# Two conditional token layers on one core: expert tables built in groups of four, and a rearranged start and end

## The reference

```
out_nr  = gelu(x @ w1_nr  + b1_nr)  @ w2_nr  + b2_nr            # condition 0
out_tsr = gelu(x @ w1_tsr + b1_tsr) @ w2_tsr + b2_tsr           # condition 1
h       = gelu(x @ w1_sr + b1_sr)          # 256 -> 512, condition 2
out_sr  = gelu(h @ w2_sr + b2_sr) @ w3_sr + b3_sr
x1 = layernorm(x + out_of_the_condition) * gamma + beta

hid = gelu(x1 @ down_W.T + down_b)                               # 256 -> 64
hid = hid @ expert_W[domain].T + expert_b[domain] + domain_emb[domain]
y   = layernorm(hid @ up_W.T + up_b + x1) * ln_gamma + ln_beta
```

## Time and profile before

| | us |
|---|---|
| median of 3 runs | 279.01 (278.82 to 284.55) |
| the profiled execution, its own time | 278.94 |
| its span, first to last instruction | 277.2 |
| TensorE busy | 262.2 (95%) |
| VectorE, ScalarE, GpSimd busy | 208.6, 207.6, 150.0 |
| mean granted TensorE clock | 0.991 |

### The profile page before, as it was taken

One profiled execution on the slowest core, in us unless ns is written; L12 is line 12 of the kernel. 1 busy time (PEld: TensorE's weight loads), 2 busy tenths in 40 slices (PEclk: granted clock), 3 DMA queues, 4 the chain that ended last, 5 costly groups with the idle time before them and its releaser, 6 DMA issues.

```text
span 277.2 us, 8503 instructions
## 1 busy us (share of the span) xinstructions
PE 262.2 (95%) x2163; PEld 242.8 (88%) x2164; DVE 208.6 (75%) x724; ACT 207.6 (75%) x490; POOL 150.0 (54%) x171
## 2 busy tenths in 40 slices
PE   8999999999999998899999999999999999999850
PEld 6688989999999997799999999999999999999640
DVE  7886241545944945989898899989889999898882
ACT  3577597687687686688888878888888888887720
POOL 3232554555656656555566655656665555565563
PEclk9999999999999999999999999999999999999996
DMA  6471210111131121132332424233242423231122
GB/s 176 132 248 38 50 41 21 23 41 25 35 78 39 37 76 42 34 95 66 85 85 66 104 67 129 69 85 85 66 104 66 124 68 92 78 93 39 59 78 79
DMA packets 44030, 20.93 MB, mean 76 GB/s; under 512 B 37783, under 2 KB 42182, under 8 KB 44008
## 3 DMA queue, kind: packets, MB, share of 16 engines
q1 hardware_dynamic: 41428, 15.21, 22.4%
q0 software_dynamic: 1584, 4.33, 4.2%
q10 hardware_dynamic: 996, 1.13, 1.5%
HBM read 11.96 MB, written 8.65 MB: 74 GB/s over the span
## 4 chain that ended last, share of the span: by engine, by line
PE 84%; DVE 7%; issue 3%; ACT 1%; DMA 1%; POOLq 0%; POOL 0%; DVEq 0%; SPq 0%; ACTq 0%
PE ps_h L1024 19%; PE ps_u L1152 11%; PE ps_z L1101 11%; PE ps_d L1167 6%; PE ps_z L1106 6%; PE ps_t L1123 5%; PE ps_u L1059 5%; PE ps_z L1059 5%; PE ps_z L1089 4%; PE ps_t L1217 3%; PE ps_u L991 3%; PE ps_t L1220 3%; PE ps_t L1218 3%; DMA per_unit_sb<-in_per_unit 1%; DVE n L694 1%
## 5 line engine op out<-in xcount | busy, mean ns | idle before, releaser
L464 POOL TENSOR_TENSOR h_lo<-h,h_hi 128x256 fp32r<-128x256 f32 (+1 forms) x75 | 69.6, 928 | 78.1 <-ACT h L850 78.0
L469 POOL TENSOR_TENSOR rs<-ve,minus_half 128x4 f32<-128x4 f32 x36 | 40.5, 1124 | 32.8 <-DVE ve L670 32.5
L850 ACT ACTIVATE h_hi<-ps_h,per_feature_sb 128x256 fp32r<-128x256 f32 x84 | 38.1, 479 | 23.0 <-PE ps_h L1024 22.2
L658 DVE BATCH_NORM_STATS2 st<-ps_z 128x6 f32<-128x256 f32 x66 | 24.9, 417 | 29.8 <-PE ps_z L1106 29.8
L486 POOL DMA_INDIRECT out<-o,out_rows_now x33 | 35.1, 1064 | 7.9 <-issue 6.2
L889 ACT ACTIVATE yt<-ps_t,per_feature_sb 128x256 f32<-128x256 f32 x66 | 34.0, 573 | 6.3 <-PE ps_t L1123 6.3
L857 ACT ACTIVATE zn<-ps_z,nm,rs 128x256 f32<-128x256 f32 x66 | 33.5, 562 | 6.2 <-DVE nm L674 6.2
L850 ACT ACTIVATE h<-ps_h,per_feature_sb 128x256 f32<-128x256 f32 x84 | 38.0, 481 | 0.0
L1152 PE MATMUL ps_u<-table_hi,stack 128*128 x132 | 35.9, 302 | 0.1
L1152 PE MATMUL ps_u<-table_lo,stack_hi 66*128 x132 | 33.0, 281 | 0.0
L1101 PE MATMUL ps_z<-last_hi,h_hi 128*128 (+1 forms) x132 | 32.6, 280 | 0.3 <-ACT h_hi L850 0.3
(11 more groups left out here) (156 smaller groups left out, 691.1 us busy)
## 6 DMA issues: line engine op xcount, KB each, us to landing
x<-in_x_feat SPq DMA_DIRECT2D x130, 64.0 KB
out<-o SPq DMA_DIRECT2D x65, 64.0 KB, 2.0
last_sb<-in_last_w SPq DMA_DIRECT2D x1, 768.0 KB, 4.7
out<-o,out_rows_now POOLq DMA_INDIRECT x33, 2.8
w_sr_sb<-in_w_sr SPq DMA_DIRECT2D x1, 512.0 KB, 4.5
w_sr_sb<-in_w_sr ACTq DMA_DIRECT2D x1, 512.0 KB, 5.8
w_two_sb<-in_w_two SPq DMA_DIRECT2D x1, 512.0 KB, 5.3
per_unit_sb<-in_per_unit ACTq DMA_DIRECT2D x1, 325.0 KB
```

What stands on the lines that cost most here:

```text
L464: pool.tensor_tensor(dst, full, high.bitcast(F32), ALU.subtract).then_inc(ready, 1)
L469: pool.tensor_tensor(RS[p][:, :, :], VE[p][:, :, :], mhalf[:, :].rearrange("p (n t) -> p n t", n=2), ALU.pow).then_inc(rstd, 1)
L850: ins = act.activation(dst[:, m, :], src[m], ACT.Gelu, bias=COL[:, bass.ds(col + m, 1)])
```

## The change

**Tables.** The host lays every expert matrix down once. A product of 128 weight columns now makes two different tables, one in partitions 0 to 63 and one in 64 to 127, and a group of two products makes four. Nine products make the 18 tables instead of 18, in five groups. `table_high` and `table_low` become two instructions of 64 partitions for each group. Even tables are then only in the lower half of `T1` and odd ones only in the upper half; in head step 1 SP issues two DMAs inside the SBUF that copy each to the other half (`s_halves_in`, waited for before the first expert product). Groups 0 to 3 are made before the loop, group 4 in step -1; their high halves are made at the start (0 to 2) and in step 0 (3, 4), the low ones at the start (0, 1), in step -1 (2) and in step 0 (3, 4).

**Start.** SP loads w1_sr ahead of the matrices of the tables. TensorE has three filler products where it had pair 0, and waits for the matrices after the positions.

**End.** Variances and powers of the two norms are made apart in the last steps. In LAST1 ScalarE normalises slot 31 between the first copies and the others, and VectorE finishes slot 28 ahead of `minus_mean`; its `stack_low` moves to LAST0. Tile 1 of slot 32 leaves by two direct stores, one from SP and one from ScalarE, in place of GpSimd's indirect one. ScalarE also issues the second direct store of slot 31.

The diff, cut to what matters:

```diff
-        EARLY_PAIRS = 5
+        GROUPS = (TE + 3) // 4
+        EARLY_GROUPS = 4
...
-        EARLY_UNIT = H + 2 * E + 2 * TABLE_BANKS * 2 * A
+        EARLY_UNIT = H + 2 * E + 4 * TABLE_BANKS * A
...
-        PAIRS_IN_STEP = {0: (5, 6), 1: (7, 8)}
-        assert TE == 2 * 9
+        MADE, HIGH, LOW = {-1: (4,)}, {0: (3, 4)}, {-1: (2,), 0: (3, 4)}
...
+            sp.dma_start(W["w1_sr"][:, :], W_DRAM["w1_sr"]).then_inc(s_w_in["w1_sr"], 16)
             sp.dma_start(UNIT[:, 0:EARLY_UNIT], per_unit[:, 0:EARLY_UNIT]).then_inc(s_unit_in, 16)
-            sp.dma_start(W["w1_sr"][:, :], W_DRAM["w1_sr"]).then_inc(s_w_in["w1_sr"], 16)
...
+                if where == HEAD and g == 1:
+                    sp.wait_ge(s_fold_hi, GROUPS)
+                    for h in range(2):
+                        own, other = slice(h * A, h * A + A), slice(A - h * A, P - h * A)
+                        sp.dma_start(T1_BY_TABLE[other, h:TE:2, :].bitcast(F32),
+                                     T1_BY_TABLE[own, h:TE:2, :].bitcast(F32)).then_inc(s_halves_in, 16)
...
 
                     rows = [rows_to_store(g - 4 + k) for k in range(4)]
-                    for k in range(4):
+                    row1 = row_of_tile1(sp, g - 1, 0)
+                    for k in range(3):
                         sp.wait_ge(o_made, g - 3 + k)
-                        store(rows[k] if k < 3 else rows[k][0:1], p if k % 2 == 0 else q)
+                        store(rows[k] if k < 2 else rows[k][0:1], p if k % 2 == 0 else q)
+                    sp.wait_ge(o1_made, g)
+                    store_half(sp, row1, q, 0, 1)
+                    sp.wait_ge(o_made, g)
+                    store_half(sp, rows[3][0], q, 0)
                     for buffer in range(2):
...
+                        sp.wait_ge(sc_out[buffer], 16 * (more + FEW // 2))
...
+                        sp.wait_ge(st_out[buffer], STORED * (more + (FEW // 2 + 2 - 2 * buffer)))
...
+            def power(count, p, norms):
+
+                pool.wait_ge(var, count)
+                pool.tensor_tensor(RS[p][:, norms, :], VE[p][:, norms, :], half_of_two[:, norms, :],
                                    ALU.pow).then_inc(rstd, 1)
+
+            def powers(g, i, p, where):
+
+                if where == LAST1:
+                    store(g, i, p, where)
+                    power(g + 2, p, FIRST)
+                elif where == LAST0:
+                    power(g + 3, p, FIRST)
+                elif where != HEAD or g >= 0:
+                    power(g + 1, p, BOTH)
...
                     rows_now(g - 4, p, i - 2)
+                    store_tile(g - 4, p, 2)
                     rows_now(g - 3, q, i - 1)
-                    store_tile(g - 4, p, 2)
                     store_tile(g - 3, q, 3)
-                    power(g + 1, q)
+                    power(g + 4, q, SECOND)
                     rows_now(g - 2, p, i - 1)
-                    power(g + 2, p)
-                    rows_now(g - 1, q, i)
+                    power(g + 5, p, SECOND)
                     store_tile(g - 2, p, 4)
-                    store_tile(g - 1, q, 5)
...
                         low(h2l[:, 0, :], h2[:, 0, :], h2h[:, 0, :], h0_full, h0_lo, g + 1)
...
+                    powers(g, i, p, where)
...
-                store(g, i, p, where)
-                if where == LAST0:
-                    power(g + 1, 1 - p)
+                if where != LAST1:
+                    store(g, i, p, where)
+                if where in SECOND_ALONE:
+                    power(SECOND_ALONE[where] + g, 1 - p, SECOND)
...
-            def table_low(j):
-                bank = table_bank(j)
-                at = slice(2 * H * j, 2 * H * (j + 1))
-                dve.wait_ge(s_fold_hi, j + 1)
-                dve.tensor_tensor(T2[0:A, at], flat(bank[0:A]), T1[0:A, at].bitcast(F32),
-                                  ALU.subtract).then_inc(s_fold_lo, 1)
-
-            table_low(0)
             weight_low("w1_sr")
...
-                for d in range(2):
-                    last = dve.tensor_copy(EXP[:, e, d * A:(d + 1) * A], ident[0:A, 0:A])
+                last = dve.tensor_copy(EXP[:, e, :], ident[0:A, 0:A])
...
+            dve.tensor_copy(ROWS1[:, :, :], row_of[:, :].rearrange(by_slot, k=G)[:, :, G // 2:G])
...
+            def table_low(j):
+                bank = table_bank(j)
+                dve.wait_ge(s_fold_hi, j + 1)
+                for h in range(2):
+                    own = slice(h * A, h * A + A)
+                    ins = dve.tensor_tensor(T2_BY_TABLE[0:A, tables(j, h), :], bank[own, 0:len(pairs_of(j)), :],
+                                            T1_BY_TABLE[own, tables(j, h), :].bitcast(F32), ALU.subtract)
+                ins.then_inc(s_fold_lo, 1)
...
-            table_low(1)
+            table_low(0)
             b_sr = slots_of_sr(dve)
             input_low(0, 0)
...
             weight_low("w2_sr")
-            for j in range(2, EARLY_PAIRS):
-                table_low(j)
+            table_low(1)
...
+
+                dve.tensor_scalar(VE[p][:, norms, :], MV[p][:, norms, :, 1], EPS, None, ALU.add).then_inc(var, 1)
...
+            def minus_mean(slot, p, where):
+                dve.wait_ge(rstd, slot + {LAST1: 2, LAST0: 3}.get(where, 1))
...
+
+            def finish(slot, i, q, where, tiles=((1, o1_made), (0, o_made))):
 
                 p = 1 - q
-                dve.wait_ge(rstd, slot + 4)
...
-                for t, ready in ((1, o1_made), (0, o_made)):
+                for t, ready in tiles:
...
-                for j in pairs(where, g):
+                for j in groups(LOW, where, g):
                     table_low(j)
...
+                if where == LAST1:
+                    first_stats(g, p)
+                    center(g - 3, q, p)
+                    first_moments(g, p)
+                    variances(p, FIRST)
+                    finish(g - 3, i - 1, q, where)
+                    last_variances(g - 2, p, q)
+                    minus_mean(g, p, where)
+                    center(g - 2, p, q)
+                    continue
+
                 if where == LAST0:
                     first_stats(g, p)
                     first_moments(g, p)
-                    variances(p)
-                    center(g - 3, q, p)
-                    minus_mean(g, p)
+                    variances(p, FIRST)
+                    stack_low(g - 2, p, True)
+                    finish(g - 3, i - 2, q, where, ((1, o1_made),))
+                    minus_mean(g, p, where)
+                    finish(g - 3, i - 2, q, where, ((0, o_made),))
                     last_variances(g - 2, p, q)
-                    finish(g - 3, i - 2, q, where)
+                    center(g - 2, p, q)
                     stack_low(g - 1, q, True)
-                    center(g - 2, p, q)
                     continue
...
-                variances(p)
+                variances(p, BOTH)
...
                 for slot in on_slot(g, 2, where):
-                    second_stats(slot, p)
-                    second_moments(slot, p, q)
+                    if where == LAST2:
+                        last_variances(slot, p, q)
+                    else:
+                        second_stats(slot, p)
+                        second_moments(slot, p, q)
...
             def table_high(j):
                 act.wait_ge(s_fold, j + 1)
-                act.copy(T1[:, 2 * H * j:2 * H * (j + 1)], flat(table_bank(j))).then_inc(s_fold_hi, 1)
+                bank = table_bank(j)
+                for h in range(2):
+                    own = slice(h * A, h * A + A)
+                    ins = act.copy(T1_BY_TABLE[own, tables(j, h), :], bank[own, 0:len(pairs_of(j)), :])
+                ins.then_inc(s_fold_hi, 1)
...
             weight_high("w1_sr")
-            table_high(0)
             act.wait_ge(s_load_ids, 1)
...
-            for j in range(1, 3):
+            for j in range(2):
...
             b_sr = slots_of_sr(act)
-            table_high(3)
...
             input_high(0, 0, 0)
             weight_high("w2_sr")
-            table_high(4)
+            table_high(2)
...
-            def adapter_gelu(slot, q, where):
+            def adapter_gelu(slot, q):
+
+                stack_high(slot, q)
+                gelu_full(q)
+
...
 
                 act.wait_ge(d_ps, slot + 1)
                 for t in range(TT):
                     own = slice(t * A, t * A + A)
                     act.activation(two_cols(S[q], t)[own], two_tokens(DP[own, 0:P]), ACT.Gelu,
                                    bias=COL[own, COL_DOWN_B:COL_DOWN_B + 1])
-                for t in range(TT) if where == LAST1 else ():
+
+            def second_high(q):
+
...
+            def gelu_full(q):
...
                 if where == DRAIN:
                     residual_norm(g - 1, q, where)
                     second_copy(g - 2, p)
-                    adapter_gelu(g - 1, q, where)
+                    adapter_gelu(g - 1, q)
                     second_copy(g - 1, q)
```

(51 more changed lines are left out.)

61 lines of the change are left out of this document (32 added, 29 removed).

## The result

The changed kernel takes **276.63 us** (median of four runs, 276.25 to 276.86), the kernel before 278.9 (278.82 and 279.01). The ratio is 0.9917, 95% interval 0.9893 to 0.9941, so 0.8% faster by a measurement that tells 0.25% from nothing. Both kernels sometimes need 5 to 8 us more, all of it ahead of slot 0; such executions are left out of every comparison, and of the profiles of after_aligned, head_shifted and after_filler, which are of that kind (last layer of slot 0 at 31.6 to 31.8 us), only lengths of stretches are read. The profiled execution after has a span of 275.1 us; 277.2 before.

A forecast was written before the change was run, and what follows sets the result against it. TensorE was taken to bound the kernel, 84% of the chain, so savings count only where it goes on sooner or another engine holds the chain; 0.6 + 1.4 + 0.3 = 2.3 us off gave 276.6 us, range 274.5 to 279.2.

The forecast's parts named there:

- last stores: After the last `O`: the direct stores issued by ScalarE, in place of GpSimd's indirect one, gain 0.1 us.
- start: Up to slot 1's first layer: earlier place and fewer low halves let TensorE start 0.6 us sooner, bounds 0 to 1.1.
- steps 0 and 1: Head steps: removing the table pairs saves 0.7 us in each, 1.4 together; the rest becomes waiting for ScalarE.
- the steps between: From step 2 to the last but three: nothing changes, as the tables keep their size and place; 0 us.
- order of the last steps: LAST1 to DRAIN: zn of slot 31 stays as late, but stack_low and the last finish come earlier; 0.2 us gained.
- from the sum to the chances: Whole time: a measurement tells about 2%, 5.6 us, from no change, so a result within 2% got 0.94.
- A: Rival at the end: minus_mean ready by 255.9, idle gap closes, indirect store ended the run; 1.7 us more, 274.9; chance 0.2.
- B: Rival at the start: longer locks or ScalarE outrunning its cover lose the 0.6 and cost 0.3; 277.5 us; chance 0.15.
- C: Rival at the start: TensorE stays at half speed through the table groups, 2.9 us more, 279.5 us; chance 0.12.
- Group 4 in step -1: Before slot 1: its one product falls where TensorE waits for GpSimd's h_lo anyway, so it costs nothing.
- cover gone: Step 0: ScalarE's four copy instructions delay slot 1's gelu beyond the roughly 3 us covering it; a possible 0.3 us loss.
- The copies: Two DMAs between table halves, 1.18 MB, finish well before the first expert product, with 16 us of room; cost 0.

The follow-up runs named there:

- after_aligned: The changed kernel with one unused 32-byte tile behind ROWS1, moving all tiles declared after it; ratio to the kernel before 0.9963.
- head_shifted: The changed tables and start with the old end, plus one unused 32-byte tile that moves the later tiles; ratio to the kernel before 0.9973.
- after_filler: The changed kernel with four filler products just ahead of TensorE's wait for h2_full in each of steps 0 and 1; ratio to the kernel before 0.9911.
- after_again: The changed kernel run and traced once more, nothing altered; ratio to the kernel before 0.9923.
- head_stores: The changed kernel with the old powers and order of the last steps, but the new direct last stores; ratio to the kernel before 0.9936.
- head_only: The changed kernel with the old stores, powers and order of the last steps; ratio to the kernel before 0.9935.
- after_placed: The changed kernel with one unused 96-byte tile behind ROWS1; ratio to the kernel before 0.9937.
- placed_guard: The changed kernel with the unused 96-byte tile and a small memset on VectorE ahead of each x_lo; ratio to the kernel before 0.9932.
- best: The changed kernel with the 96-byte tile, group 4 made in step 0 and low halves of groups 3 and 4 in step 1; ratio to before 0.9917.
- best_at64: The changed kernel with a 224-byte tile, group 4 made in step 0, low halves of groups 3 and 4 in step 1; ratio to before 0.9916.
- end_placed: The kernel before with the changed end and the unused 96-byte tile; ratio to the kernel before 1.0000.
- best_guard: The changed kernel with 224-byte tile, group 4 in step 0, low halves 3 and 4 in step 1, memset ahead of x_lo; ratio 0.9901, median 275.99 us.
- after_mean_first: The changed kernel with minus_mean moved ahead of last_variances in LAST1; ratio to the kernel before 0.9988.

## Why the prediction was right and wrong

**The time** was forecast at 276.6 and is 276.63, inside the range of 274.5 to 279.2, but partly by luck: last stores that paid more than forecast made up for head steps that paid less and for a loss that was missing. With the other profiled executions each term has its own figure (number of executions in brackets):

| term | forecast | measured | from |
|---|---|---|---|
| start | 0.6 | 0.6 | first product of slot 1: mean 20.21 with the old start (3), 19.62 with the new (14) |
| steps 0 and 1 | 1.4 | 0.8 | last layer of slot 2: mean 46.95 and 45.57, 1.4 less, of which 0.6 is the start's |
| the steps between | 0 | -0.7 | 21 steps, 127.97 against 128.69 |
| order of the last steps | 0.2 | 0.4 | slot 32 to the last `o`: 17.46 (old, 4) against 17.04 (after, after_again); 17.50 in head_stores |
| last stores | 0.1 | 1.0 | last `o` to the end: 4.63 (4) against 3.60 (13, 3.21 to 4.32) |
| sum | 2.3 | 2.1 | ratio 0.992: 2.3 |

**The step that failed** is the one from the sum to the chances: "a measurement of this kernel can tell about 2%, 5.6 us, from no change", and with it 0.94 for no change. The forecast of 2.3 us was itself 0.8%, and the interval of the ratio is 0.24% to either side: the time fell by 0.8%, clear of no change, which the text had given 0.94. The median of the kernel before came out at 278.8 to 279.3 each time. By the text's own cases nearly all of A, B and the forecast lay beyond the 0.7 us that can be told; the chance of faster should have been some 0.8. The three runs shown (278.82, 279.01, 284.55) looked like a spread of 2%, but the first two agree within 0.1%.

Within the sum, three terms were mis-sized: steps 0 and 1 (1.4, measured 0.8), the steps between (0, measured a loss of 0.7) and the last stores (0.1, measured 1.0).

**Start** (0.6; 0.42 in the profile after, 0.59 between the means). C is refuted by the 0.91 us; even in head_only, head_stores and after_placed, where the full rate came latest, only the first two or three records of the groups were slow. `place` gave 0.27 (TensorE's next product at 6.55, before at 6.82). The sum has a slip: it took the end of `x_lo`, 19.6, for TensorE's start, which comes 0.14 later, so its own working gives 0.47. The lock moved from `last_b_lo` to `x_lo` as argued in the profile after and three more of the fourteen; in the other ten, after_again among them, `h_lo` is first, `last_b_lo` takes 1.38 to 1.50 us and `x_lo` 0.67 to 0.69. It makes no difference: placed_guard, one of the ten, starts slot 1 at 19.76. Group 4 in step -1 ("nothing") stands on the chain in after, but is not what is missing: best and best_at64, which make it elsewhere, gain no more than 0.05 us there. VectorE's `x_lo`, which ended at 19.58 in after, would have held TensorE next. What moves the start from one execution to the next is when TensorE's full rate came: eight of the new start that had it by 6.6 us start slot 1 at 19.18 to 19.51, the three that got it latest, at 9.5 us or after, at 20.33 to 20.48. The one execution of the old start that had it early, end_placed, stands at 19.80.

**Steps 0 and 1** (1.4, measured 0.8): 0.71 twice behind the middle layer, by the mechanism foreseen, and the filler shows that it is ScalarE's wait. But other stretches of step 1 got longer. The last layer of slot 1 came 11.05 and 11.03 us after that of slot 0 before; it comes 10.60 to 10.64 after it in the four kernels of the new start at 64, and 10.79 to 10.82 in those at 96, the changed one among them. So 0.42 of the 0.7 is left at equal position, and the position takes 0.18 more. Of the 0.3 that is missing, 0.2 stands at the last layer of slot 0: its low products take 0.66 us in the chain, 0.47 before, since GpSimd's `h_lo` ends only at 25.76 and they begin at 25.82. The text had allowed 0.1. What it put as a possible 0.3 (cover gone) did come in part, by another way: `nm` locked out for 1.25 us, then `zn` of slot 0 a microsecond late, for which TensorE waits 0.2 us ahead of the residual of slot 2 in head_only. VectorE's low halves are not the cause of that lock: moved away in best, best_at64 and best_guard, they left `nm` at 1.25 to 1.27, and end_placed, with the old start, has 1.27 too. In all of these, as in after, the power ahead of `nm` began 0.16 us or more behind `x_lo` and took 1.42 to 1.50 instead of 1.04. Why `x_lo` comes first there stays open.

**The copies:** two DMAs of 576 KB, landed 6.3 us after their issue near 29 us, and the first expert product near 44 us waits for none. 0, as forecast; leaving them out wasn't tried.

**Order of the last steps** (0.2, measured 0.4): `minus_mean` no earlier, as argued (256.13, before 255.55), and rival A's closed gap was not to be had: after_mean_first started the transposes 0.5 us sooner and lost time. **Last stores** (0.1): here the mis-sized term. I took the direct store's landing as the end and the indirect one as hidden, because it was issued 0.07 us earlier. In fact SyncE's wait for it was the last (2.5 us, now 1.6 for a direct one), and the program's end took 1.0 us more, by the chain on GpSimd's queue, now 0.2 to 0.6. That half of rival A ("the indirect store was what ended the run") is what happened.

**The steps between** were "nothing changes: the tables have the same size and place". The tables have; the tiles behind ROWS1 don't.

## What to carry to other kernels

Set the bound for "no change" by how closely repeated runs agree, not by the distance from the lowest to the highest. Compare the length of the steps that a change does not touch before you credit or blame it: here a 288-byte tile cost a third of what the whole change brought, and one of 224 bytes behind it took that back in the trace. When moved work stands on the chain, ask what would end next without it: group 4 stood there, and taking it away moved nothing. A saving behind one wait has to be followed to the next one, whose cover it may have been. And of the last stores, ask which one the queue at the very end is waiting for, not which was issued last.

## What the runs showed that I had not expected

TensorE's products of 256 columns take 279 to 283 ns by where `x` and `h` lie within 256 bytes, up to 1.3 us over 21 steps, with nothing idle. GpSimd's power of four columns takes 1.04 us when it begins 0.01 us or more before VectorE's `x_lo`, and 1.60 when both begin together. A power of two columns took 0.69 to 1.02. And TensorE's full rate came anywhere between 4.2 and 9.9 us in executions of like kernels, behind the same filler products, which moves the last layer of slot 0 between 23.9 and 25.1 us with the new start.
